# Latent projections with keys and queries halved before they are turned, and routed rows without their weight

## The reference

```
# layer 1 attention: 77 context tokens ask, 1024 tokens and the 77 answer; 16 heads of 64
xn, ln = layernorm(x), layernorm(latents)
q, k, v = ln @ Wq, [xn; ln] @ Wk, [xn; ln] @ Wv        # inner width 1024
k = k / norm(k, per head) * kn_g;  q = q / norm(q) * qn_g
x = x + softmax(q @ k.T) @ v @ Wout + bout

# layers 1 and 3, experts: each token goes to the one of 8 experts with the largest probability
probs = softmax(tokens @ gate_w)
e, weight = argmax(probs), max(probs)
x[t] = x[t] + weight[t] * (act(xn[t] @ w1[e]) @ w2[e])  # act is relu in layer 1 (at most
                                                        # 320 tokens an expert), gelu in layer 3
```

## Time and profile before

| what | us |
|---|---|
| median of 3 runs | 3302.73 |
| lowest and highest run | 3302.71, 3307.28 |
| the profiled execution, its time | 3319.2 |
| the profiled execution, its span | 3317.5 |
| TensorE (PE) busy in the span | 2831.8 |
| DVE busy | 2282.6 |
| ACT busy | 2054.2 |
| POOL busy | 1351.6 |

### The profile page before, as it was taken

How to read it: one execution, slowest core, us unless ns; L and a number is a source line. 1 busy time by engine, 2 the same in 40 slices (tenths; PEclk the granted TensorE clock), 3 DMA queues, 4 the chain that set the end, 5 groups by cost and what they waited for, 6 DMA issues and landing times. The chain is left out here.

```text
span 3317.5 us, 69921 instructions
## 1 busy us (share of the span) xinstructions
PE 2831.8 (85%) x27561; PEld 1935.8 (58%) x27561; DVE 2282.6 (69%) x3443; ACT 2054.2 (62%) x3053; POOL 1351.6 (41%) x975
## 2 busy tenths in 40 slices
PE   6769998765969998969998587879999999989578
PEld 3246665424436666536665477666666666657467
DVE  6968887678868884769996344767555565558545
ACT  3448887274748886648887122666666666548256
POOL 2249998120238886118887032550000000018132
PEclk8979999887979999979999788988999999999689
DMA  3411111200322220325553966011222222154876
GB/s 130 175 57 53 56 54 57 103 13 13 102 44 55 55 55 24 100 61 156 156 156 113 152 230 205 8 33 52 77 77 77 77 77 77 51 176 106 60 204 196
DMA packets 244890, 309.01 MB, mean 93 GB/s; under 512 B 140265, under 2 KB 186647, under 8 KB 231511
## 3 DMA queue, kind: packets, MB, share of 16 engines
q1 hardware_dynamic: 229789, 250.44, 28.1%
q0 software_dynamic: 12544, 51.67, 4.6%
q10 hardware_dynamic: 2233, 2.39, 0.2%
HBM read 198.47 MB, written 68.64 MB: 81 GB/s over the span
## 5 line engine op out<-in xcount | busy, mean ns | idle before, releaser
L2685 POOL TENSOR_TENSOR lta_p_lo<-lta_p,lta_p_hi 128x1024 f16<-128x1024 f32 x256 | 556.2, 2203 | 178.6 <-DVE lta_p_hi L2808 178.2
L2884 ACT ACTIVATE lta_p<-lta_banks,lw_gmax 128x512 f32<-128x512 f32 x512 | 323.9, 683 | 94.7 <-PE lta_banks L2723 91.3
L2791 DVE TENSOR_REDUCE lta_s_ps<-lta_s_ps 128x1 f32<-128x1101 f32 x240 | 313.9, 1308 | 83.8 <-PE lta_s_ps L2701 83.8
L4783 PE MATMUL m_y_ps<-m_w,m_hT 128*128 128x256 f16 x3072 | 355.8, 273 | 1.8 <-DVE m_hT L4943 1.8
L4771 PE MATMUL m_h_ps<-m_x,m_w 128*128 128x512 f16 x1536 | 353.6, 380 | 3.3 <-issue 3.3
L4868 ACT ACTIVATE m_h<-m_h_ps,m_h_bias,m_h_scale 128x512 f32<-128x512 f32 x256 | 199.4, 779 | 231.1 <-PE m_h_ps L4771 222.9
L4783 PEld LDWEIGHTS m_y_ps<-m_w,m_hT 128*128 128x128 f16 x3072 | 299.2, 98 | 64.8 <-issue 7.6
L4943 DVE TENSOR_TENSOR m_hT<-m_h,m_hT 128x512 f16<-128x512 f32 x256 | 176.1, 691 | 200.3 <-ACT m_hT L4868 196.4
L1234 POOL TENSOR_TENSOR c0a_tri_p_lo<-c0a_tri_p,c0a_tri_p_hi 128x1024 f16<-128x1024 f32 (+2 forms) x192 | 285.7, 1524 | 57.9 <-DVE c0a_tri_p_hi L1408 57.1
L4771 PEld LDWEIGHTS m_h_ps<-m_x,m_w 128*128 128x128 f16 x1536 | 150.6, 98 | 160.1 <-issue 6.3
L1483 ACT ACTIVATE c0a_tri_p<-c0a_banks,c_size 128x512 f32<-128x512 f32 (+3 forms) x384 | 208.4, 577 | 45.3 <-PE c0a_banks L1302 34.0
(11 more groups left out here) (858 smaller groups left out, 6637.5 us busy)
## 6 DMA issues: line engine op xcount, KB each, us to landing
m_w<-rp_w SPq DMA_DIRECT2D x23, 1024.0 KB
m_w<-pw_w SPq DMA_DIRECT2D x23, 1024.0 KB
ltp_pieces<-in_L_ffn_w_dram SPq DMA_DIRECT2D x16, 1024.0 KB, 5.3
lw_room<-in_L_ffn_w_dram SPq DMA_DIRECT2D x16, 1024.0 KB, 7.8
rp_w<-lw_room SPq DMA_DIRECT2D x16, 1024.0 KB, 5.3
m_raw<-in_L_ffn_W_dram SPq DMA_DIRECT2D x16, 1024.0 KB, 6.5
pwo_raw<-in_L_ffn_w_dram POOLq DMA_DIRECT2D x16, 1024.0 KB, 7.7
pw_w<-pwo_pair POOLq DMA_DIRECT2D x16, 1024.0 KB, 4.5
```

The source lines that it names most:

```text
L2685: nc.gpsimd.tensor_tensor(p_lo[:, slot, :], p32[:, p32_slot(h, j), :], p_hi[:, slot, :], ALU.subtract).then_inc(rested, 1)
L2791: nc.vector.tensor_reduce(ntop_of(h)[:, n:n + 1], scores(h, n), AX_X, ALU.max, negate=True).then_inc(top_ready, 1)
L2884: nc.scalar.activation(p32[0:rows, slot, c * 512:(c + 1) * 512], t_ps[0:rows, c, :], ACT.Exp, bias=bias, scale=p["gmax"][0:rows, 0:1]).the ...
L4783: last = nc.tensor.matmul(y_ps[:, q, 0:D], hT[:, k % 2, a, f, q * P:(q + 1) * P], w2[:, v, b, f, :], start=f == 0 and m == 0, stop=f == FC ...
```

## The change

It has three parts.

A routed row has 512 numbers (ROW = 2*D), 2048 bytes in place of 2052. The store of the weights into the rows and the waits for it are gone.

A row's weight is found by product instead: DVE splits the weights in three bf16 parts, multiplies each with `tile_hot` (which of the 23 tiles a token goes to), and TensorE adds them up by lane with 16 matmuls of 69 columns. DVE adds the three parts to `share`. In layer 3 the last token of each expert, which fills up empty places, needs its share as well: one more small matmul and a few operations. In layer 1 `share` is multiplied into `y_back` once.

In `latent_project` keys and queries are halved before the turn. DVE's `scale` writes `qk` as before; for keys POOL multiplies it by the key factors laid out in a row (`gain`); ACT makes the f16 high part of the 128x1024 rows (`halve`), POOL the rest (`split_side`); TensorE turns both as f16, 16 transposes instead of 8 for each of queries and keys (`turn_side`), and ACT (`keep_high`) and DVE (`keep_low`) copy them out of PSUM. Keys are turned a step later than before (s-3 instead of s-2), queries in the same step but after the first half of the values. The blocks measured by ACT have one buffer (`piece`).

```diff
@@ latent_project
-    qk = sb("qk", [P, 2, INNER])
+    qk, qk16 = sb("qk", [P, 2, INNER]), sb("qk16", [P, 2, 2, INNER], F16)
-    t_ps, v_ps, x_ps = ps("t_ps", [P, INNER]), ps("v_ps", [P, 512]), ps("x_ps", [P, 2, DC, P], F16)
+    t_ps, v_ps, x_ps = ps("t_ps", [P, 2, INNER], F16), ps("v_ps", [P, 512]), ps("x_ps", [P, 2, DC, P], F16)
...
+        def gain(n):
+            rows = rows_of(n)
+            pool.wait_ge(scaled[K], n + 1)
+            keys = by_head(qk[0:rows, K, :])
+            nc.gpsimd.tensor_tensor(keys, keys, p["gain_row"][0:rows, :].unsqueeze(1).to_broadcast([rows, H, DH]), ALU.mult).then_inc(gained_k, 1)
+
+        def split_side(n, k):
+            rows = rows_of(n)
+            pool.wait_ge(halved[k], n + 1)
+            if n:
+                pool.wait_ge(turned[k], 2 * n)
+            nc.gpsimd.tensor_tensor(qk16[0:rows, k, 1, :], qk[0:rows, k, :], qk16[0:rows, k, 0, :], ALU.subtract).then_inc(split[k], 1)
...
-        for n in range(LAST + 1):
-            affine(n)
-            rest(n)
+        for s in range(STEPS):
+            if within(s - 2):
+                gain(s - 2)
+            if within(s):
+                affine(s)
+                rest(s)
+            if within(s - 2):
+                split_side(s - 2, K)
+            if within(s - 1, Q):
+                split_side(s - 1, Q)
         if b == 0:
             weights.fill_constants(pool, filled)
...
+        def keep_low(n, k):
+            rows = rows_of(n)
+            dve.wait_ge(turned[k], 2 * n + 2)
+            nc.vector.tensor_copy((qT, kT)[k][:, 1, :, n * P:n * P + rows],
+                                  t_ps[:, 1, :].rearrange("p (c t) -> p c t", c=PAIRS)[:, :, 0:rows]).then_inc(kept_lo[k], 1)
...
         every = kT[:].rearrange("p a i n -> p (a i) n")
-        dve.wait_ge(rested[K], 2 * (LAST + 1))
+        dve.wait_ge(kept_hi[K], LAST + 1)
+        dve.wait_ge(kept_lo[K], LAST + 1)
...
+        def halve(n, k):
+            rows = rows_of(n)
+            if k == Q:
+                act.wait_ge(scaled[k], n + 1)
+            else:
+                act.wait_ge(gained_k, n + 1)
+            if n:
+                act.wait_ge(turned[k], 2 * n - 1)
+                act.wait_ge(split[k], n)
+            nc.scalar.copy(qk16[0:rows, k, 0, :], qk[0:rows, k, :]).then_inc(halved[k], 1)
...
+            for part, (ready, kept) in enumerate(((halved, kept_hi), (split, kept_lo))):
+                pe.wait_ge(ready[k], n + 1)
+                if k == K and 0 <= n + 1 < LAST:
+                    pe.wait_ge(kept[Q], n + 2)
+                elif k == K:
+                    pe.wait_ge(kept[K], n)
+                elif n == 1:
+                    pe.wait_ge(kept[Q], 1)
+                elif n > 1:
+                    pe.wait_ge(kept[K], n - 1)
+                for c in range(PAIRS):
+                    last = nc.tensor.transpose(t_ps[:, part, c * P:c * P + rows], qk16[0:rows, k, part, c * P:(c + 1) * P],
+                                               p["ident"][0:rows, 0:rows])
+                last.then_inc(turned[k], 1)
...
-ROW = 2 * D + 1
+ROW = 2 * D
...
-        sp.wait_ge(weighted, 1)
-        sp.dma_start(by_tile[:, :, 2 * D:2 * D + 1], weight[:].unsqueeze(2), allow_slow_non_contiguous=True).then_inc(w_stored, 16)
         if pairs is None:
-            sp.wait_ge(w_stored, 16)
...
-        pool.wait_ge(w_stored, 16)
         pool.wait_ge(ids_ready, 1)
...
+        pe.wait_ge(shared, 3)
+        for t in range(TILES):
+            last = nc.tensor.matmul(share_ps, lane_hot[:, t, :], share_marks[:, t].rearrange("p a n -> p (a n)"),
+                                    start=t == 0, stop=t == TILES - 1)
+        if capacity is None:
+            pe.wait_ge(final_ready, 2)
+            last = nc.tensor.matmul(last_share_ps, env.ones[:], last_token[:], start=True, stop=True)
+        last.then_inc(shares_found, 1)
...
+        step(nc.vector.tensor_copy(share[:, :, 0], weight[:]))
+        tt(rest[:], weight[:], share[:, :, 0], ALU.subtract)
+        step(nc.vector.tensor_copy(share[:, :, 1], rest[:]))
+        tt(share[:, :, 2], rest[:], share[:, :, 1], ALU.subtract)
+        for k in range(3):
+            nc.vector.tensor_tensor(share_marks[:, :, k, :], tile_hot[:], share[:, :, k:k + 1].to_broadcast([P, TILES, NT]),
+                                    ALU.mult).then_inc(shared, 1)
         for table, out in tables:
             tt(product[:], mine[:], table[:].unsqueeze(1).to_broadcast([P, NT, E]), ALU.mult)
             reduce(out[:], product[:], ALU.add)
+        if capacity is None:
+            tt(cand[:], final[:], over_e(weight), ALU.mult)
+            nc.vector.tensor_reduce(last_token[:], cand[:].rearrange("p t e -> p e t"), AX_X, ALU.max).then_inc(final_ready, 1)
+            dve.wait_ge(shares_found, 1)
+            tt(product[:], mine[:], last_share_ps.unsqueeze(1).to_broadcast([P, NT, E]), ALU.mult)
+            reduce(fill[:], product[:], ALU.add)
+            tt(fill[:], fill[:], empty[:], ALU.mult)
+        dve.wait_ge(shares_found, 1)
+        step(nc.vector.tensor_copy(r["share"][:], share_ps[:, 0:NT]))
+        tt(r["share"][:], r["share"][:], share_ps[:, NT:2 * NT], ALU.add)
+        tt(r["share"][:], r["share"][:], share_ps[:, 2 * NT:3 * NT], ALU.add)
```

More of the change, by code:

```diff
@@ L2235, in join_gains @@
         step(nc.vector.reciprocal(small[:], p["gmax"][:]))
+        step(nc.vector.tensor_scalar(p["gain_row"][:], both, small[:, 0:1], None, ALU.mult))
         step(nc.vector.tensor_tensor(p["gain"][:], p["gain"][:], small[:], ALU.mult))
@@ L2306, in latent_project @@
     v_done, v_halved, v_split, table_loaded = (sem(n) for n in ("v_done", "v_halved", "v_split", "table_loaded"))
-    pieces, piece_loaded, measured = sb("pieces", [P, 2, RoutedPairs.WIDE]), [sem(f"piece_loaded{u}") for u in range(2)], sem("measured")
+    piece, piece_loaded, measured = sb("piece", [P, RoutedPairs.WIDE]), sem("piece_loaded"), sem("measured")
     MINE = RoutedPairs.PIECES // B
     pair = lambda n: tuple(sem(f"{n}_{x}") for x in "qk")
-    done, squared, summed, rooted, floored, inverted, scaled, turned, halved, rested = (
-        pair(n) for n in ("done", "squared", "summed", "rooted", "floored", "inverted", "scaled", "turned", "halved", "rested"))
+    done, squared, summed, rooted, floored, inverted, scaled, halved, split, turned, kept_hi, kept_lo = (
+        pair(n) for n in ("done", "squared", "summed", "rooted", "floored", "inverted", "scaled", "halved", "split", "turned", "kept_hi", "kept_lo"))
+    gained_k = sem("gained_k")
     block = ctx.enter_context(nc.Block())
@@ L2324, in _ @@
         for i in range(MINE):
-            if i >= 2:
-                sp.wait_ge(measured, i - 1)
-            routed.load(sp, MINE * b + i, pieces[:, i % 2, :], piece_loaded[i % 2])
+            if i:
+                sp.wait_ge(measured, i)
+            routed.load(sp, MINE * b + i, piece[:], piece_loaded)
     @block.gpsimd
@@ L2386, in scale @@
             if n:
-                dve.wait_ge(turned[k], 2 * n)
+                dve.wait_ge(split[k], n)
             nc.vector.tensor_tensor(by_head(qk[0:rows, k, :]), by_head(side_ps[k][0:rows, :]),
                                     rn[0:rows, k, :].unsqueeze(2).to_broadcast([rows, H, DH]), ALU.mult).then_inc(scaled[k], 1)
-        def rest(n, k, half):
+        def keep_low(n, k):
             rows = rows_of(n)
[L2394 to L2400, removed]
+            dve.wait_ge(turned[k], 2 * n + 2)
+            nc.vector.tensor_copy((qT, kT)[k][:, 1, :, n * P:n * P + rows],
+                                  t_ps[:, 1, :].rearrange("p (c t) -> p c t", c=PAIRS)[:, :, 0:rows]).then_inc(kept_lo[k], 1)
         def split_values(n, half):
@@ L2478, in halve_values, with keep_high @@
                 nc.scalar.activation(value_heads(n, half, 0), by_head(v_ps[:]), ACT.Identity, scale=p["v_scale"][:, 0:1]).then_inc(v_halved, 1)
[L2480 removed]
+        def halve(n, k):
             rows = rows_of(n)
[L2482 to L2485 removed]
+            if k == Q:
[6 more added lines that the diff above has]
+            nc.scalar.copy(qk16[0:rows, k, 0, :], qk[0:rows, k, :]).then_inc(halved[k], 1)
+        def keep_high(n, k):
+            rows = rows_of(n)
+            act.wait_ge(turned[k], 2 * n + 1)
+            nc.scalar.copy((qT, kT)[k][:, 0, :, n * P:n * P + rows],
+                           t_ps[:, 0, :].rearrange("p (c t) -> p c t", c=PAIRS)[:, :, 0:rows]).then_inc(kept_hi[k], 1)
         for s in range(STEPS):
```

116 lines of the change are left out of this document (50 added, 66 removed).

## The result

| kernel | median us | ratio to before | 95% interval |
|---|---|---|---|
| before | 3302.72 (3300.67 to 3307.28, 4 runs) | | |
| changed | 3364.05 (3359.66 to 3365.45, 4 runs) | 1.0182 | 1.0164 to 1.0199 |

The change costs 61.3 us where 45 were forecast. That is inside the range of 3315 to 3378, but above the likeliest case's own range of 3340 to 3358. The profiled execution of the changed kernel took 3365.45, the longest of its four, 1.4 above the median. Against the profiled execution of before (3319.2) that is +46.3.

The account below looks back on a forecast made before the run. Latent projections were bound by PE and DVE work, routings by a wait for stores. The latent stage's +93 us and the routings' -47.8 summed to +45, 3348 us, range 3315 to 3378.

Parts of the forecast that it names:

- the likeliest case: Whole kernel: the forecast of 3348 us, own range 3340 to 3358, chance 0.36.
- The ring: Latent projections: a closed round of waits across PE, ACT and DVE sets the period, 14.7 us a tile instead of 10.30.
- The clock: Latent projections: PE's clock falls under 1.00, adding 1.0 us a tile for a period of 15.7; 14 us in all.
- POOL or the clock costs its full price: Latent projections, rival: a period of 16.5 gives 11 us more, 3359 us; chance 0.09.
- the clock stays up: Latent projections, rival: PE's clock holds, period 14.7, 14 us less, 3334 us; chance 0.22.
- The gain: Latent projections: POOL's new multiplication of the keys takes 2.2 us, between 1.87 and 2.9.
- The term of 0.25 for the floors: Latent projections: POOL's work beside DVE's 16-column floor operations adds 0.25 us a tile to the round.
- Filling the pipeline: Latent projections: a pipeline one operation deeper costs about 2 us for each batch, 4 us in all.
- Ends: Latent projections, end of each batch's block: +4.5 us with b = 1, +8.8 us with b = 0.
- The routings: Layer 1's first fetch 20.0 us earlier and layer 3's first product 27.8 us earlier, together -47.8 us.
- Both rivals on the stores: Routings' row stores: they stay slow, 3376 us, chance 0.15; or get a little faster, 38.5 becoming 34.2, 3367 us, chance 0.05.
- The step that failed: Whole kernel: the profiled 3319.2 us stands 0.5% above the median, so the median becomes 3302.7 + 45 = 3348 us.

Follow-up runs that it names:

- the shorter loop: The latent change alone with each engine's list in another order, no operation removed; 3324.13 us, and 3316.13 with normalise moved behind the sum of the keys.
- the routings alone: The kernel before with only rows of 512 numbers and weights by product, the latent projections unchanged; 3263.76 us, ratio 0.9883.
- the latent change alone: The kernel before with only the diff's part ahead of the routings, the latent projections, changed; 3398.27 us, ratio 1.0291.

## Why the prediction came out as it did

**The ring.** Right in place and size. Taking the clock out leaves 14.74 against 14.7; a round of the changed kernel in which the clock held is 935.96 - 921.14 = 14.82. (The first round, 14.62, doesn't count: no keys are turned in it yet, so the ring isn't closed.) Lengthening a link lengthened the round by its length, lengthening POOL's work did not, and another order broke it.

**The clock.** Right in kind, too small. Rounds of the changed kernel took 16.6 (b = 0) and 15.8 (b = 1), a mean of 16.2 against 15.7, nearer to the rival "POOL or the clock costs its full price" (16.5) than to my own term. A round takes 14.7 to 14.8 where the clock holds and 16.4 to 19.3 where it falls; the forecast of 14 us for it should have been near 21, of which keeping PE busy recovered 19.6 in the rounds and 13.7 in all. The rival "the clock stays up" is out.

**POOL and the shared ports.** The gain took 2.35, between my 1.87 and 2.9, above the 2.2 taken. The term of 0.25 for the floors was right. On the ring stands the floor of the queries, and it took 0.54 beside POOL's gain where that of the keys, with POOL idle, took 0.23:

```profile
920.59 0.23 DVE L2400 TENSOR_SCALAR ltp_rn<-ltp_rn,lw_floor 128x16 f32<-128x16 f32 x1 [0.28 <-ACT ltp_rn L2481]
...
924.28 0.54 DVE L2400 TENSOR_SCALAR ltp_rn<-ltp_rn,lw_floor 128x16 f32<-128x16 f32 x1 [0.28 <-ACT ltp_rn L2481]
```

That is 0.31 a round. No floor took over 1 us, as I had said some would; the longest took 0.72. The larger delay was one that I didn't name: `normalise` was held to 1.78 in nearly every tile, off the ring. In the shorter loop the same wait came onto the path and cost 8 us until it was moved. The Trainium skill ("SBUF — State Buffer", section "SBUF: two separate sides") has the pair of ports that DVE and GpSimd share as an exclusive lock for a whole instruction, and the trace agrees: `normalise` takes 0.40 alone and 2.26 beside POOL's split, and ends just behind it.

**Ends.** Filling the pipeline: with b = 0, from the block's first operation to the first scale of keys 21.2 us instead of 17.9, and 1.4 less in the last round, so about 2 net, as forecast. Ends +4.6 (b = 1) and +9.1 (b = 0), forecast 4.5 and 8.8. In all +95.8 for the stage against 93. The clock's missing 7 us don't show in full, partly because before was not at 10.30 in all of its rounds either: seven of them took 74.3 and 72.3 us, not 72.1.

**The routings.** Lined up at the ids, the changed kernel's profiled execution is ahead of that of before by 19.4 us at layer 1's first fetch and by 26.3 at layer 3's first product; forecast 20.0 and 27.8. In layer 3 I was near the number with the wrong last link. I had DVE's tail and copy come last and took the 8.55 from fetch to product over from before. DVE's copy ended at 3219.40, but PE first had to turn the rows of two tiles, which it got at 3219.06 and 3221.10, so the fetches came last, and the product stood 11.22 behind the first of them. That the number is off by only 1.5 is luck. In before, the three loads of expert weights (`m_w`) were issued long ahead of the fetch; now they are issued within 2.1 us of it. That they slow the fetches was not tested. Both rivals on the stores are out: the last landings fell to 3.0, not to 34. From the rule of the Trainium skill ("DMA: Bandwidth & Descriptors", section "How a descriptor splits into AXI transactions"), that a transaction starts at a 256-byte boundary and the bytes ahead of the start cost beats, the prediction had worked out an estimate of one part in eight more. That is far below the landings, which were six (18.6 against 3.0) to thirteen times as long, though those contain queueing. The prediction also put the 36.8 of the weights down to their place in the queue; 2048 such writes with nothing ahead of them took 23.5.

**The step that failed** is the one from the profile to the median: "it stands 0.5% above the median, which becomes 3302.7 + 45 = 3348". It took the surplus of the profiled execution as a constant added to both kernels. But 10.5 of its 16.5 us were the very waits that the change removes, drawn long in that execution. In usual runs the routings give 38.7, not 47.8, and this is the larger part of the miss. The clock's term is the smaller one. With 38.7 and the stage's measured 95.8 the sum is +57. The remaining 4 us up to the measured 61.3 are hardly more than the medians scatter. In the profiled executions they lie ahead of layer 1's ids: the routings alone reach these 4.5 us earlier than before (1876.59 against 1881.10), the whole change no earlier than the latent change alone (1977.74 against 1977.69). Why is open.

## What to carry to other kernels

Sum the work of each engine, but then walk the orders of all engines for a closed ring, in which every operation waits for the one before it in the round. If it is longer than the work of the busiest engine, its length is the period. Here another order of the same operations was worth 74 us, and one operation moved behind another 8 more.

Rows in DRAM with an odd word at their end can be worth padding: here a pitch of 2304 bytes was as good as 2048 and far better than 2052, with the extra word left where it was. Other pitches weren't tried.

When the profiled execution is slower than the median, find out in which waits before a gain measured in it is carried over; a second profile of the same kernel tells.

## What the runs showed of the hardware

A store of 512 KB in pieces of 1 KB to DRAM (layer 1's last block) landed in 3.0 us at a pitch of 2048, in 3.3 at 2304, and at 2052 in 18.6 without small writes near it and in 38.5 with them behind it, other blocks queued ahead in both. 2048 writes of 4 bytes took 3.9 at a pitch of 2304 and 23.5 at 2052, with nothing ahead of them, and the loads behind them in the queue took up to 23.2.

Matmuls with no use, put where TensorE waits, raised its granted clock in the loop from 0.86 to 1.00 (b = 0) and made the program 13.7 us shorter.
